# Feature attention of an eight-layer kernel run as one software pipeline over sequences, with its weights loaded in the first layer, its output matrices merged, and unread products in the norm stages

## What is computed

```
td = einsum('bhnd,md->bhnm', t * dn, proj)      # t is q or k; H=16 heads of DH=8, M=16 features, dn = 8**-0.25
diag = 0.5 * dn ** 2 * jnp.sum(t * t, axis=-1, keepdims=True)
mx = max over m (queries), or over n and m (keys)
f = ratio * (jnp.exp(td - diag - mx) + EPS)      # qp for queries, kp for keys
d_inv = 1.0 / einsum('bhnm,bhm->bhn', qp, sum_n(kp))
context = einsum('bhnm,bhnd->bhmd', kp, v)
out = einsum('bhmd,bhnm,bhn->bhnd', context, qp, d_inv)
h = out @ Wo.T + bo
x = x + jax.nn.relu(h @ Wfc.T + bfc)
```

## Time and profile before

| what | us |
|---|---|
| median of 3 timed runs | 3333.71 (3332.17 to 3342.23) |
| the profiled execution, its own time | 3327.2 |
| its span in the trace | 3325.0 |
| feature attention, from the end of the DVE instruction before it to the end of its last one | 549.98 to 787.18, so 237.20 |
| PE busy over the span | 2861.7 (86%) |
| DVE, ACT, POOL busy | 1684.6, 1505.1, 1367.1 |
| mean granted TensorE clock over the span | 0.908 of full |

### The profile page before, as it was taken

The page is one execution under the profiler, slowest core; times in us unless marked ns, Lnnn a source line. Parts: engine busy times, 40 slices in busy tenths (PEclk is TensorE's granted clock), DMA queues, the critical chain, the costliest instruction groups (busy, mean ns, idle before and its releaser), DMA issues. The chain is left out here.

```text
span 3325.0 us, 45251 instructions
## 1 busy us (share of the span) xinstructions
PE 2861.7 (86%) x14231; PEld 1822.8 (55%) x14258; DVE 1684.6 (51%) x4152; ACT 1505.1 (45%) x3006; POOL 1367.1 (41%) x1231
## 2 busy tenths in 40 slices
PE   6877995776767888874995999999999998899998
PEld 4566994665653333334992444444444444677776
DVE  4445445564326999985223555555555555211111
ACT  3431332221227777741323665666566564344443
POOL 0012772111566998962323555555555555000000
PEclk9876997775787999995996999999999998799999
DMA  5002673000451222212003000000000000000000
GB/s 157 0 26 87 204 206 103 1 0 26 129 144 56 78 74 77 77 54 80 25 18 114 1 1 0 0 0 0 0 0 0 0 1 1 13 13 6 13 6 25
DMA packets 97985, 151.11 MB, mean 45 GB/s; under 512 B 14307, under 2 KB 50934, under 8 KB 97830
## 3 DMA queue, kind: packets, MB, share of 16 engines
q1 hardware_dynamic: 87206, 127.88, 12.4%
q0 software_dynamic: 10240, 20.99, 2.8%
q10 hardware_dynamic: 384, 0.46, 0.1%
HBM read 132.18 MB, written 25.50 MB: 47 GB/s over the span
## 5 line engine op out<-in xcount | busy, mean ns | idle before, releaser
L1445 POOL TENSOR_TENSOR l3a_p<-l3a_p,l3a_rden 128x512 f32<-128x512 f32 x512 | 521.0, 1040 | 487.0 <-DVE l3a_rden L1484 483.9
L1474 DVE CUSTOM_DVE_ANT_0 l3a_p<-bank,l3a_bias 128x512 f32<-128x512 f32 x512 | 333.8, 689 | 200.2 <-PE bank L1623 186.9
L1544 ACT ACTIVATE l3a_p<-l3a_p,l3a_low 128x512 f32<-128x512 f32 x512 | 365.5, 719 | 12.6 <-DVE l3a_low L1474 12.6
L1632 PEld LDWEIGHTS bank<-ident,l3a_p 128*128 128x128 f32 x2048 | 228.1, 140 | 167.3 <-issue 158.0
L2219 POOL TENSOR_TENSOR l2a_dBu<-l2a_du,l2a_bs 128x1024 f32<-128x1024 f32 x128 | 299.2, 2351 | 33.9 <-DVE l2a_h L2443 32.8
L1550 ACT COPY l3a_pT<-bank 128x512 f32<-128x512 f32 x256 | 150.2, 587 | 321.3 <-PE bank L1632 320.9
L2443 DVE TENSOR_TENSOR_SCAN l2a_h<-bank,l2a_dBu 128x1024 f32<-128x1024 f32 x128 | 290.4, 2280 | 8.7 <-ACT bank L2350 8.7
L1623 PE MATMUL bank<-l3a_kT,l3a_qT 64*128 64x512 f32 x1024 | 291.1, 644 | 1.4 <-DVE l3a_low L1474 0.7
L1632 PE MATMUL bank<-ident,l3a_p 128*128 128x128 f32 x2048 | 275.8, 277 | 3.0 <-DVE l3a_pT L1480 2.3
L849 DVE SCALAR_TENSOR_TENSOR x<-bank,l3f_gates,x 128x128 f32 x256 | 85.5, 351 | 371.1 <-PE bank L877 371.1
L877 PEld LDWEIGHTS bank<-l3fe_w,l3fe_h 128*128 128x128 f32 x2048 | 233.8, 192 | 15.3 <-issue 15.3
(11 more groups left out here) (488 smaller groups left out, 4820.8 us busy)
## 6 DMA issues: line engine op xcount, KB each, us to landing
l2a_bs<-l2a_b_rows SPq DMA_DIRECT2D x128, 256.0 KB, 3.0
l0fe_wi<-in_L_ffn_in_dram SPq DMA_DIRECT2D x40, 516.0 KB
l0fe_wo<-in_L_ffn_out_dram SPq DMA_DIRECT2D x40, 320.0 KB, 3.4
by_place<-by_distance SPq DMA_DIRECT2D x16, 512.0 KB, 13.7
l1fe_wo<-in_L_ffn_out_dram SPq DMA_DIRECT2D x24, 320.0 KB, 3.3
l3a_bias<-by_place SPq DMA_DIRECT2D x16, 448.0 KB, 13.0
l1fe_wi<-in_L_ffn_in_dram SPq DMA_DIRECT2D x24, 258.0 KB
l0fe_answers<-l0f_y_rows SPq DMA_DIRECT2D x16, 256.0 KB, 5.2
```

Of the source, the lines that this page charges most:

```text
L1445: ins = pool.tensor_tensor(a, a, rden[:, t, h:h + 1].to_broadcast([P, S]), ALU.mult)
L1474: bk.drain(dve.tensor_tensor_reduce(p[u % 2][h][:, t, :], ps(job)[:], bias[:, u % HP * 2 + h, b0:b0 + S], 1.0, 3.0e38, ALU.add, ALU.min, l ...
L1544: ins = act.activation(a, a, ACT.Exp, bias=low[h][:, t:t + 1], scale=-1.0, accum_out=den[:, t, h:h + 1])
L1632: ins = pe.transpose(ps(job)[:, t * P:(t + 1) * P], p[u % 2][h][:, t, kt * P:(kt + 1) * P], chip.ident[:])
```

## The change

Four things are changed.

1. **Norm stages.** In `normalise_and_route` PE now issues four products of 512 columns (`keep_running(4)`: `ident` times the first four tiles of `x`, into bank 2) before it waits for anything, and one such product ahead of each later sequence. Nobody reads bank 2 in the stage. This holds for all five norm stages, so for 55 products.
2. **Weights of feature attention.** One array `packed` of 128 rows by 1020 columns takes the place of the fourteen inputs. SP loads it in the first layer, between the scan's weights and `prepare_later_layers`, and POOL makes `feat` and the scaled biases there.
3. **Merged output matrices.** `fold` multiplies `wo` and `wfc` once (`out_w`), and `fold_bias` carries the bias of v and of the output through. The product with `wo` per sequence, its copy on ACT and the bias addition to v go away.
4. **The pipeline.** The two turns with four sequences become one unrolled loop of ten steps. In step i PE works on the features of sequence i, the projections of i+1, the transposes, context and weighing of i-1 and the output of i-2. The features of keys sit in banks 0 and 1 and those of queries in 2 and 3, one sequence at a time (`f_taken` says that DVE has taken them); banks 4 to 7 take the rest. DVE does the whole subtraction in one pass per kind over 1024 columns, since the largest key feature is now in the subtrahend (`subtrahends`) before it; the 32 instructions of L1877 go away. `xn` moves to POOL, whose rstd comes from `ALU.pow` in place of a square root on ACT and a reciprocal on DVE. The copies of q and k move from DVE to ACT, and so does that of v. The division takes two instructions per sequence and not eight.

```diff
+                def keep_running(n):
+                    for _ in range(n):
+                        pe.matmul(chip.psum[2][:], chip.ident[:], chip.x[:, 0:TPS, :].rearrange("p t d -> p (t d)"), start=True, stop=True)
+                keep_running(4)
                 if NR:
                     pe.wait_ge(loaded, 16)
                 for i in range(B if (turned_out or NR) else 0):
+                    if i:
+                        keep_running(1)
...
+    def load(self, sp, w):
+        sp.dma_start(self.packed[:], w["packed"]).then_inc(self.loaded, 16)
...
+    def prepare(self, pool):
+        pool.wait_ge(self.loaded, 16)
+        pool.tensor_tensor(self.feat[:], bcast(self.head_of, n_after=self.M), bcast(self.proj, n_before=H1), ALU.mult)
+        pool.tensor_scalar(self.scaled_bias[:, 0:1], self.bq, float(DH1) ** -0.25, 0.0, ALU.mult, ALU.add)
+        pool.tensor_scalar(self.scaled_bias[:, 1:2], self.bk, float(DH1) ** -0.25, 0.0, ALU.mult, ALU.add).then_inc(self.prepared, 1)
...
+        f_banks = [chip.banks[:, 2 * n:2 * n + 2, :] for n in range(2)]
+        order = [(("out_w",), 7), (("out_b",), 7), (("xT", 0), 4), (("k", 0), 5), (("q", 0), 6), (("v", 0), 7)]
+        for i in range(B + 2):
+            order += [(("oT", i - 2), 4)] if i >= 2 else []
+            order += [(("most", i), 6)] if i < B else []
+            order += [(("xT", i + 1), 7)] if i + 1 < B else []
+            order += [(("y", i - 2), 5)] if i >= 2 else []
+            order += [(("less", i), 6)] if i < B else []
+            order += [(("k", i + 1), 4)] if i + 1 < B else []
+            order += [(("fT", i - 1, 0), 7), (("fT", i - 1, 1), 5)] if 1 <= i <= B else []
+            order += [(("q", i + 1), 6)] if i + 1 < B else []
+            order += [(("cx", i - 1), 7)] if 1 <= i <= B else []
+            order += [(("v", i + 1), 5)] if i + 1 < B else []
+            order += [(("o", i - 1, 0), 4), (("o", i - 1, 1), 6)] if 1 <= i <= B else []
...
-                for t, n in ((wq, "Wq"), (wk, "Wk"), (wv, "Wv"), (wo, "Wo"), (wfc, "Wfc"), (proj, "proj"),
-                             (head_of, "head_of"), (half_head, "half_head"), (own, "own")):
-                    sp.dma_start(t[:], w[n]).then_inc(weights, 16)
-                for t, n in ((bq, "bq"), (bk_, "bk"), (bo, "bo")):
-                    sp.dma_start(t[:], w[n].rearrange("(p o) -> p o", o=1)).then_inc(weights, 16)
-                for t, n in ((bv, "bv"), (bfc, "bfc")):
-                    sp.dma_start(t[:], w[n].partition_broadcast(P)).then_inc(weights, 16)
...
+                def shift(q):
+                    job = ("less", q)
+                    bk.wait_filled(dve, job, 0)
+                    a = ps(job)[:, 0:2 * TPS * H].rearrange("p (n t h) -> p n t h", n=2, h=H)
+                    dve.tensor_tensor(less[QUERIES][q % 2][:], most[QUERIES][q % 2][:], a[:, QUERIES], ALU.add)
+                    bk.drain(dve.tensor_copy(less[KEYS][q % 2][:], a[:, KEYS]), job)
+                    bk.wait_read(dve, job, 0)
+                    for n in (QUERIES, KEYS):
+                        dve.tensor_tensor(f[n][q % 2][:].rearrange("p t h m -> p (t h) m"), f_banks[n].rearrange("p b (a m) -> p (b a) m", m=M),
+                                          bcast(less[n][q % 2][:].rearrange("p t h -> p (t h)"), n_after=M), ALU.subtract).then_inc(f_taken[n], 1)
...
+                for i in range(B + 2):
+                    if i < B:
+                        largest_keys(i)
                         for c2 in range(2):
+                            ins = largest(i, QUERIES, c2)
+                        c.link(ins)
+                        largest_of_all(i)
+                    if i >= 2:
+                        add(i - 2)
+                    if i < B:
+                        shift(i)
+                    if i + 2 < B:
+                        statistics(i + 2)
+                    if 1 <= i <= B:
+                        keep_own(i - 1)
+                        for c2 in range(2):
+                            divide(i - 1, c2)
...
+                    c.link(pool.tensor_scalar(var[:, cut], mv[:, cut, 1], LN_EPS, 0.0, ALU.add, ALU.add))
+                    c.link(pool.tensor_tensor(rstd[:, cut], var[:, cut], minus_half[:].to_broadcast([P, TPS]), ALU.pow))
+                    chip.apart(pool)
+                    for t in range(TPS):
+                        n = q * TPS + t
+                        ins = pool.tensor_scalar(xn[q % 2][:, t, :], chip.x[:, n, :], mv[:, n, 0:1], rstd[:, n:n + 1], ALU.subtract, ALU.mult)
...
+                pool.wait_ge(minus_half_ready, 1)
+                normalise(0)
+                normalise(1)
+                for n in (KEYS, QUERIES):
+                    square(0, n)
+                for i in range(B):
+                    if i + 1 < B:
+                        square(i + 1, KEYS)
+                    affine(i, QUERIES)
+                    if i + 1 < B:
+                        square(i + 1, QUERIES)
+                    affine(i, KEYS)
+                    if i + 2 < B:
+                        normalise(i + 2)
...
+                act.wait_ge(held.prepared, 1)
+                bk.wait_filled(act, ("out_w",), 0)
+                act.activation(mid_b[:], ps(("out_w",))[:, D:D + 1], ACT.Identity, bias=held.bo).then_inc(mid_ready, 1)
+                bk.drain(act.copy(out_w[:], ps(("out_w",))[:, 0:D]), ("out_w",))
+                act.wait_ge(mid_ready, 1)
+                act.activation(mid_rows[:], chip.ones[:], ACT.Identity, scale=mid_b[:]).then_inc(rows_ready, 1)
+                take_turned(("xT", 0), xnT[0][:])
...
+                for i in range(B + 2):
+                    if i >= 2:
+                        take_turned(("oT", i - 2), oT[i % 2][:])
+                    if i + 1 < B:
+                        take_turned(("xT", i + 1), xnT[(i + 1) % 2][:])
+                        take_projected(i + 1, KEYS)
+                    if 1 <= i <= B:
                         for c2 in range(NCH):
+                            take_turned(("fT", i - 1, c2), fT[(i - 1) % 2][:, c2, :])
+                    if i < B:
+                        exponential(i, QUERIES)
+                    if i + 1 < B:
+                        take_projected(i + 1, QUERIES)
+                    if i < B:
+                        exponential(i, KEYS)
+                    if i + 1 < B:
+                        take_values(i + 1)
...
+                def fold():
+                    bk.wait_drained(pe, ("out_w",), 0)
+                    pe.matmul(ps(("out_w",))[:, 0:D], held.wo, held.wfc, start=True, stop=True)
+                    bk.fill(pe.matmul(ps(("out_w",))[:, D:D + 1], held.wo_turned, held.bv, start=True, stop=True), ("out_w",))
+                def fold_bias():
+                    pe.wait_ge(rows_ready, 1)
+                    bk.wait_drained(pe, ("out_b",), 0)
+                    bk.fill(pe.matmul(ps(("out_b",))[:, 0:D], mid_rows[:], held.wfc, start=True, stop=True), ("out_b",))
...
+                for i in range(B + 2):
+                    if i < B:
+                        features(i, KEYS)
+                    if i >= 2:
+                        turn_answer(i - 2)
+                    if i < B:
+                        features(i, QUERIES)
+                        turn_most(i)
+                    if i + 1 < B:
+                        turn(i + 1)
+                    if i >= 2:
+                        give_out(i - 2)
+                    if i < B:
+                        subtrahends(i)
+                    if i + 1 < B:
+                        project(i + 1, KEYS)
+                    if 1 <= i <= B:
+                        turn_queries(i - 1)
+                    if i + 1 < B:
+                        project(i + 1, QUERIES)
+                    if 1 <= i <= B:
+                        context(i - 1)
+                    if i + 1 < B:
+                        values(i + 1)
+                    if 1 <= i <= B:
+                        weigh(i - 1)
...
+                layer(chip, part(prefix), held, part("L2_attn_"), features, part("L1_attn_"))```

How the order on PE changes in feature attention. Before, this is the end of a turn; `fq`, `fk` are the features, `cx` the context, `fT` the turned query features, `o` the answer:

```order
L2011 MATMUL bank<-l1a_v,l1a_fk 128x65 x16
L98 REGISTER_ALU
L2011 MATMUL bank<-l1a_v,l1a_fk 128x65 x16
L2024 MATMUL bank<-l1a_cx,l1a_fT 128x72 x24
L78 REGISTER_ALU
L2024 MATMUL bank<-l1a_cx,l1a_fT 128x72 x8
L2032 MATMUL bank<-ident,l1a_o 128x128 x12
L78 REGISTER_ALU
L2032 MATMUL bank<-ident,l1a_o 128x128 x4
L2037 MATMUL bank<-l1a_oT,l1a_wo 128x512 x4
L2042 MATMUL bank<-l1a_wfc,l1a_hT 128x128 x16
```

518 lines of the change are left out of this document (246 added, 272 removed).

## The result

| | kernel before | kernel changed |
|---|---|---|
| median of the runs, us | 3336.97 (3332.17 to 3342.23, 4 runs) | 3240.16 (3239.25 to 3249.25, 4 runs) |
| profiled execution, us | 3327.2, span 3325.0, clock 0.908 | 3249.25, span 3247.5, clock 0.933 |

The ratio is 0.9711, 95% interval 0.9698 to 0.9724: 96.8 us faster. The forecast of 3226 was 14 us too low: inside the 3205 to 3252 that got a chance of 0.82, and at the upper edge of the likeliest case's own 3218 to 3240. So the traces show only 77.5 us: feature attention 236.9 to 167.0 (from its first statistics to those of the next stage), the five norm stages 13.0 together, and some 5 given back in the stages between.

The account below looks back on a forecast made before the run. PE was taken as the busiest engine, partly at half clock, with no engine filling feature attention. From 3327.2, less 92 (feature attention) and 12 (norm stages), came 3223; 3 added gave 3226 us, range 3205 to 3252 (likeliest 3218 to 3240).

Parts of the forecast that it names:

- the likeliest case: Whole kernel: pipeline bound by PE, clock mostly full, norm products warm; 3218 to 3240 us, chance 0.50.
- Feature attention saves 92: Feature attention: 237.2 us becomes 138.8, less 6 of the saving for clock falls; 92 saved, range 63 to 98.
- The step that failed: POOL in feature attention: `ALU.pow` taken as 0.3 us, hidden under 9 us of slack, shown once at the start.
- PE's work of 14.6 and the step of 14.9: Feature attention: PE's work per sequence at full clock 14.6 us; a middle step 14.9, set by PE's queue.
- The clock's falls, 0.8 per step: Feature attention: a fall in every second step costing 1.6 us, so 0.8 per step and 6 in all.
- Norm stages, 12 saved: Norm stages: 2.5 us saved in each of four with a router, 2 through l3a; 12 together, range 5 to 16.
- The early load on no path: First layer: the big weight load in SP's queue and POOL's preparation there delay nothing on the path.
- The added 3 us: Whole kernel: half of the 6.5 us by which the runs' median 3333.7 lay above the profiled execution, added to 3223.
- Case 3: Feature attention: more waits between the queues, 2 to 3 us a step, eight steps cost 20; 3246 us, chance 0.08.
- case 4: Feature attention: half the pipeline at the half clock, step 19.5 us; 3255 us in all, chance 0.09.
- cases 5 and 6: Half clock held in norm stages by added products: 3299 us, chance 0.06; there and in the pipeline: 3409, chance 0.03.
- case 2: Clock never falls in the pipeline, rises at once in norm stages: 98 and 15 saved, 3217 us; chance 0.20.

Follow-up runs that it names:

- the pipeline alone: The changed kernel without the unread products in the norm stages: 3252.61 us, ratio 0.9745 to the kernel before.
- the second: Second profile of the changed kernel, run once more unaltered on another chip: 3292.86 us, ratio 0.9717 to the kernel before.
- (6): The changed kernel with POOL's `xn` as multiply and add, in place of subtract then multiply: 3285.51 us, ratio 0.9703 to the kernel before.
- 9: The changed kernel with POOL's normalisation earlier and in multiply-add form, and seven unread products in the last three steps: 3226.82 us, ratio 0.9665 to the kernel before.
- Experiment 7: The changed kernel with seven unread 512-column products in feature attention's last three steps: 3236.54 us, ratio 0.9703 to the kernel before.
- 11: The changed kernel with feature attention's weights loaded and prepared at its own start, not in the first layer: 3241.81 us, ratio 0.9711 to the kernel before.

## Why the prediction was right in sum, and where it was wrong

- **Feature attention saves 92: in size wrong, in kind right.** The traces show 69.9 here and 73.3 in the pipeline alone; by medians the pipeline alone saved 85. The forecast stage of 144.8 (138.8 and 6 for the clock) was 167.0. The difference of 22.2 lies in three terms: the start and step 0 (26.4 from the barrier on, 22.8 forecast), step 1 (23.9, not 13.6) and the end (37.4, not 27.9); 2 of the 6 us for the clock belong to those. Steps 2 to 6 came out as forecast in this profile, 79.3 against 74.5 + 5 x 0.8 = 78.5, and at 85.2 in the second.
- **The step that failed: the power "hides under 9 us of slack and shows once, at the start", in a POOL total of 5.9 us.** Three things in it were wrong. The power costs 1.03, about my upper bound and not 0.3. `xn` costs 3.13 for a sequence, since I took L545's duration for an instruction of another form (6). POOL is busy 8.57 in 16 us of the middle, not 5.9. And the slack was counted in busy time, where what counted was the place in the queues: `normalise(i + 2)` stands behind both affine passes, the first of which waits for ACT's exponential of the queries (1.45 in step 1), and its statistics stand behind both subtractions of DVE. The wait for `xn` that I did not list cost 8.4 us of PE's time directly, with clock falls behind that of step 1; and at the start the first `xn` took POOL 4.7 us, where the sum had 2.6. Mended in 9, step 1 is 14.4, near the 13.6 of the walk.
- **PE's work of 14.6 and the step of 14.9: right.** At full clock without waits a step takes 14.7 in the kernel of 9, all of it busy. The wait for the diagonal closed as said.
- **The clock's falls, 0.8 per step: the right size for steps 2 to 6** (three of five steps 1.7 longer in 9, so 1.0 per step; in the changed kernel one fall of five in one profile and five of five in the other). No run shows what decides whether a step falls. The end was the miss. I had priced 14.5 us for the last two sequences at full clock, and PE ran 29 us at 0.50. Experiment 7 shows that wide products put there raise the clock, but not that their lack is the cause: the same end ran partly at 1.00 in other profiles. The granted clock of the stage was 0.81 and not over 0.9.
- **The rule of the Trainium skill** (TensorE: Matmul & The Clock Gate, What's actually happening), by which a busy PE has 2.4 GHz: the trace disagrees again. In 9 PE was busy for 16.40 of 16.40 us and showed 0.90, with falls inside.
- **Norm stages, 12 saved: right.** 13.0 in the traces, 14 alone. 2.19 us per sequence was forecast as 2.2. The parts were off in opposite ways: 3.7, 3.1 and 3.6 in three stages with a router rather than 2.5, and in l3a 0.7, not 2. The following attention's first product still took 2.05, as the changed kernel's timeline of PE shows, the row that answers to the earlier trace rows:

```profile
1703.50 2.05 PE L1606 MATMUL bank<-l3a_xnT_all,l3a_w_qk 128*128 128x512 f32 x2 [2.44 <-issue]
```

- **The early load on no path:** right; PE folds at 549.83, 0.7 us behind the first statistics. That it is also worth little came out in 11. **The DVE step near 11.5:** 10.8 to 11.0 busy of 16.00, right.
- **The added 3 us** between profile and median: the median of before turned out 9.8 above its profiled execution, and that of after 9.1 below its own. Against the profiled execution the forecast was 26 us short (3223 and 3249.25): 22 in feature attention and 5 in stages forecast as unchanged, less 1 in the norm stages. The medians took 12 of them back. That the sum stayed in its range is to that extent luck.
- **Rivals.** Case 3 (more waits between the queues, 3246) comes nearest to what happened, but the queue was POOL's, not DVE's. The lower clock of case 4 came too, but in step 1 and at the end, not as a middle step of 19.5. The norm products never ran at half for long, so cases 5 and 6 fell; case 2 fell with the falls in the middle steps.

## What to carry to other kernels

In a pipeline written out by hand, slack is not busy time subtracted from the step: walk each engine's queue and ask behind which wait the needed instruction stands, and when its own inputs are ready; here a normalisation came 5.3 us late on an engine that had just been idle for 10, since both it and its statistics stood late in their queues. Take a duration from a row only if its operations match too, and price an unknown small instruction at its upper bound where its engine feeds the bottleneck. After a wait is removed, look at the granted clock before counting the gain, and at more than one profile: taking out waits worth 4 us left the five steps 2.4 us shorter on the mean.
